# Attention and a routed feed-forward layer on one core: both norms applied by ScalarE, a router product on both weight parts at once, a new order of the attention blocks, and the last block's work between the first expert tiles

## The reference

```
x = x + xattn(layernorm(x), ctx)          # 16 heads of 32, softmax over the 154 context rows
x = x + moe(layernorm(x))                 # 8 experts of 512 x 512, the 2 best of each token

xattn: q = x Wq^T + bq; k, v = ctx Wk^T + bk, ctx Wv^T + bv
       softmax(q k^T / sqrt(32)) v, then Wo^T + bo
moe:   softmax(x W_router^T + b_router), its 2 largest weights kept,
       sum over these two of weight * (x W_e^T + b_e)
```

## Time and profile before

| | us |
|---|---|
| median of the runs | 1371.55 |
| the profiled execution | 1366.51 |
| its span, first to last instruction | 1364.8 |
| PE busy | 1227.5 (90%) |
| DVE busy | 860.4 (63%) |
| POOL busy | 883.1 (65%) |
| ACT busy | 636.1 (47%) |
| mean granted clock of TensorE | 0.953 |

### The profile page before, as it was taken

The page is one execution under the profiler, slowest core; times in us unless marked ns, Lnnn a source line. Parts: engine busy times, 40 slices in busy tenths (PEclk is TensorE's granted clock), DMA queues, the critical chain, the costliest instruction groups (busy, mean ns, idle before and its releaser), DMA issues. The chain is left out here.

```text
span 1364.8 us, 37333 instructions
## 1 busy us (share of the span) xinstructions
PE 1227.5 (90%) x11552; PEld 743.6 (54%) x11553; DVE 860.4 (63%) x1905; ACT 636.1 (47%) x914; POOL 883.1 (65%) x1124
## 2 busy tenths in 40 slices
PE   5696899999998999899999997777899999999997
PEld 3352666665665656666566565443455555555553
DVE  3363687877787678687688676744455555555544
ACT  2204557546655645754754753512333343433333
POOL 5112467878878878878878966966544555454445
PEclk9787899999999989999999998888999999999999
DMA  8814456537647647656654655677999999899786
GB/s 238 224 35 128 116 152 193 188 119 232 200 127 226 179 137 221 173 166 191 193 181 126 209 156 164 243 278 185 245 178 171 173 175 175 167 168 179 143 160 120
DMA packets 136024, 240.07 MB, mean 176 GB/s; under 512 B 18533, under 2 KB 49509, under 8 KB 134757
## 3 DMA queue, kind: packets, MB, share of 16 engines
q1 hardware_dynamic: 102432, 160.67, 40.1%
q0 software_dynamic: 29952, 67.73, 24.4%
q10 hardware_dynamic: 3525, 10.06, 2.0%
HBM read 113.34 MB, written 101.71 MB: 158 GB/s over the span
## 5 line engine op out<-in xcount | busy, mean ns | idle before, releaser
L1778 PE MATMUL S<-we_s,wq_s 128*128 x1632 | 379.5, 383 | 13.9 <-DVE wq_s L1734 5.8
L1711 POOL DMA_INDIRECT out<-xn,to x136 | 210.6, 1549 | 210.1 <-DMA out<-xn,to 80.6
L1111 POOL TENSOR_TENSOR we_s<-P_s,we_s 128x1024 f16<-128x1024 f32 x112 | 239.3, 2155 | 51.2 <-ACT we_s L876 25.5
L1778 PEld LDWEIGHTS S<-we_s,wq_s 128*128 128x128 f16 x1632 | 159.2, 99 | 183.6 <-issue 24.7
L1722 ACT ACTIVATE wq_s<-PVp 128x512 f16<-128x512 f32 x138 | 82.1, 596 | 238.6 <-PE PVp L1768 238.3
L925 DVE TENSOR_REDUCE mx_sb<-S 128x6 f32<-128x924 f32 x160 | 170.9, 1110 | 2.1 <-PE S L684 2.1
L702 PE MATMUL W<-wo_s,aT_hi 128*128 128x512 f16 x512 | 162.7, 384 | 3.6 <-DVE xR_s L935 2.1
L667 PE MATMUL W<-we_s,wq_s 128*128 128x512 f16 x512 | 162.2, 389 | 3.2 <-DVE we_s L913 1.6
L1202 POOL DMA_INDIRECT dispatched<-xn,idx x128 | 126.6, 989 | 47.6 <-issue 46.7
L1756 DVE SCALAR_TENSOR_TENSOR att<-S,be_s 128x512 f32<-128x512 f32 x136 | 94.1, 692 | 97.9 <-PE S L1778 97.0
L768 PE MATMUL PVp<-Vr,we_s 128*128 128x132 f16 x768 | 92.9, 234 | 42.9 <-POOL we_s L1111 42.2
(11 more groups left out here) (190 smaller groups left out, 2038.0 us busy)
## 6 DMA issues: line engine op xcount, KB each, us to landing
P_s<-dispatched SPq DMA_DIRECT2D x140, 260.5 KB, 3.6
we_s<-we_s SPq DMA_DIRECT2D x192, 128.0 KB, 4.0
be_s<-in_x SPq DMA_DIRECT2D x16, 1024.0 KB, 9.7
xR_s<-in_x SPq DMA_DIRECT2D x16, 1024.0 KB, 6.1
out<-xR_s SPq DMA_DIRECT2D x16, 1024.0 KB, 10.4
wst<-in_weT SPq DMA_DIRECT2D x16, 512.0 KB, 7.5
we_scratch<-wsp SPq DMA_DIRECT2D x16, 512.0 KB, 6.9
Kst<-k_scratch SPq DMA_DIRECT2D x16, 480.0 KB, 5.7
```

The source lines that it names most:

```text
L1111: e.tensor_tensor(Pst[1][:, r:r + 2, :], exps(n), Pst[0][:, r:r + 2, :], ALU.subtract).then_inc(pldp, 1)
L1711: e.indirect_dma_start(out, bass.IndirectOffsetOnAxis(ap=to[u][:, :], axis=0), yw[u % YW], None, bounds_check=N - 1, oob_is_err=False, com ...
L1778: m = e.matmul(Yp[:, u % 2, :], gT[u % 2][xp][:, k, :], we_s[:, bass.ds(n * WN + (wp * KC + k) * D, D)], start=(c == 0), stop=(c == 11))
```

## The change

Six things are done:

1. `NA` is removed from POOL. `act_apply` does the same on ACT, one instruction for each tile of tokens (`NX0` to `NX3` for the first norm, `NY0` to `NY3` for the second), with scale and offset as operands. The semaphore `nap` now counts four for each block, and the scatters also wait for it.
2. `LA` multiplies the high part of the input with both parts of the weights at once, 16 columns wide, and the low part with the high weights, 8 wide: 32 matmuls in place of 48. `RA` scales both halves, and `RC` adds them instead of copying.
3. `BX` is called once for each tile of tokens, so that its four instructions can stand apart.
4. All five slot lists, `BANK` and `HOLDERS` are replaced. The slot of PE now begins at `Q10`.
5. `EARLY` is 13: the first table is made one block earlier and covers 12 turns and not 13.
6. `Oe1` to `Oe3`, `SN`, `NC`, `RQ`, `NY`, `O3` to `O11` of the last block and the scatters of the last two are taken out of the slots and put between the first tiles, over two turns. SP loads four tiles before the last expert weights, and writes the empty rows one in each turn from the third to the tenth.

```
-EARLY = 14
+EARLY = 13
...
-    def pool_norm_apply(e, n, b, src, dst):
-        e.wait_ge(nco[n], b.at(NCO, NCO))
-        hold(e)
-        for j in range(NJ):
-            i = e.tensor_scalar(dst[:, j, :], src[:, j, :], nrm[n][:, 5, j:j + 1], nrm[n][:, 6, j:j + 1], ALU.mult, ALU.add)
-        i.then_inc(nap[n], 1)
+    def act_apply(e, n, b, j, src, dst):
+        e.wait_ge(nco[n], b.at(NCO, NCO))
+        e.activation(dst[:, j, 0:D], src[:, j, :], ACT.Identity, scale=nrm[n][:, 5, j:j + 1],
+                     bias=nrm[n][:, 6, j:j + 1]).then_inc(nap[n], 1)
...
         for j in range(NJ):
-            seqs = [t for k in range(KC) for t in split3(k)]
-            for n, (xp, wp, k) in enumerate(seqs):
-                m = e.matmul(W[:, bank, j * NE:(j + 1) * NE], xnT[xp][:, k, j * P:(j + 1) * P], wr_s[:, wp, k, :], ...
+            o = W[:, bank, j * 2 * NE:(j + 1) * 2 * NE]
+            for k in range(KC):
+                e.matmul(o.rearrange("p (l e) -> p l e", l=2), xnT[0][:, k, j * P:(j + 1) * P], wr_s[:, :, k, :], start=(k == 0), stop=False)
+            for k in range(KC):
+                m = e.matmul(o[:, 0:NE], xnT[1][:, k, j * P:(j + 1) * P], wr_s[:, 0, k, :], start=False, stop=(k == KC - 1))
```

The start of the expert stage, the part of PE:

```
-            slots(e, pe_slot, -2, 2, 4)
+            slots(e, pe_slot, -3, 1, 4)
+            for i in range(3, 6):
+                pe_O(e, LAST, i, LAST + (-(-2)))
             e.wait_ge(ld_t[0], 16)
+            e.wait_ge(nmd, 4 * NB)
+            pe_turn_rows(e, 0, 0)
+            pe_turn_rows(e, 0, 1)
+            for i in range(6, 12):
+                pe_O(e, LAST, i, LAST + (-(-2)))
             e.wait_ge(ld_ew, 16 * (NE + 1))
...
-            pe_LB(e, LAST, LAST + (-(-1)))
-            for u in range(TU):
+            pe_tile(e, 0, 0)
+            pe_LB(e, LAST, LAST + (-(-2)))
+            for u in range(1, TU):
                 pe_tile(e, 0, u)
-                if u == 3:
-                    pe_R(e, LAST, LAST + (-(-2)))
+                if u == 5:
+                    pe_R(e, LAST, LAST + (-(-3)))
```

More of the change, by code:

```diff
@@ L1179, in pool_RW, with pool_BX @@
         ch.end()
[L1181 to L1193, removed]
+    def pool_BX(e, b, j):
+        if b.first and j == 0:
             e.wait_ge(L["bo"], 48)
[L1195 to L1198 removed]
+        if j == 0:
+            e.wait_ge(ld_xR[b.par], b.half(16, 16))
+            hold(e)
+        e.tensor_tensor(xR[b.par][:, j, :], xR[b.par][:, j, :], bo_b[:, :], ALU.add).then_inc(p_bx, 1)
     def scatter(e, p, k):
@@ new lines, in pe_slot @@
+        if on_bm1:
+            pe_ST(e, bm1, 7, s)
+            pe_ST(e, bm1, 8, s)
+        if on_bp1:
+            pe_XT(e, bp1, 1, s)
+            pe_XT(e, bp1, 2, s)
+        if on_bm1:
+            pe_PV(e, bm1, 2)
+            pe_PV(e, bm1, 3)
+            pe_ST(e, bm1, 9, s)
+        if on_bm3 and not bm3.last:
+            pe_R(e, bm3, s)
+        if on_bm2 and not bm2.last:
+            pe_O(e, bm2, 3, s)
+        if on_bp1:
+            pe_XT(e, bp1, 3, s)
+        if on_bm2 and not bm2.last:
+            pe_O(e, bm2, 4, s)
+            pe_O(e, bm2, 5, s)
@@ new lines, in pe_slot @@
+        if on_b:
+            pe_MX(e, b, 0, s)
+            pe_MX(e, b, 1, s)
+        if on_bm2 and not bm2.last:
+            pe_O(e, bm2, 6, s)
+        if on_bp1:
+            pe_Q(e, bp1, 0, s)
+        if on_b:
+            pe_MX(e, b, 2, s)
+        if on_bp1:
+            pe_Q(e, bp1, 1, s)
+        if on_b:
+            pe_MX(e, b, 3, s)
+        if on_bm2 and not bm2.last:
+            pe_O(e, bm2, 7, s)
+        if on_b:
+            pe_MX(e, b, 4, s)
+        if on_bm2 and not bm2.last:
+            pe_O(e, bm2, 8, s)
@@ new lines, in pe_slot @@
+        if on_b:
+            pe_MX(e, b, 5, s)
+        if on_bp1:
+            pe_Q(e, bp1, 2, s)
+        if on_b:
+            pe_MX(e, b, 6, s)
+        if on_bm1:
+            pe_PV(e, bm1, 4)
+        if on_b:
+            pe_MX(e, b, 7, s)
+        if on_bp1:
+            pe_Q(e, bp1, 3, s)
+        if on_b:
+            pe_MX(e, b, 8, s)
+        if on_bm2 and not bm2.last:
+            pe_O(e, bm2, 9, s)
+        if on_b:
+            pe_MX(e, b, 9, s)
+        if on_bm2 and not bm2.last:
+            pe_O(e, bm2, 10, s)
@@ L1300, in pe_slot @@
+        if on_b:
+            pe_MX(e, b, 10, s)
+        if on_bm2 and not bm2.last:
+            pe_O(e, bm2, 11, s)
+        if on_bm1:
+            pe_PV(e, bm1, 5)
+        if on_b:
+            pe_MT(e, b, s)
+        if on_bp1:
+            pe_Q(e, bp1, 4, s)
+            pe_Q(e, bp1, 5, s)
+        if on_bm2 and not bm2.last:
+            pe_LB(e, bm2, s)
+        if on_bm1:
+            pe_PV(e, bm1, 6)
+        if on_b:
+            pe_ST(e, b, 0, s)
             pe_ST(e, b, 1, s)
@@ L1402, in pe_slot @@
[L1402 to L1432 removed]
+            act_EX(e, b, 1)
@@ L1532, in dve_slot @@
             dve_SN(e, bm1, 0)
-        if on_bm2 and not bm2.last:
-            dve_RE(e, bm2)
         if on_bp2:
```

458 lines of the change are left out of this document (213 added, 245 removed), and 8 rows, old and new, of the table BANK.

## The result

The changed kernel is slower by 1.5%: 1389.68 us median of four runs (1388.23 to 1396.53) against 1372.94 (1371.31 to 1376.96) of the kernel before beside it, ratio 1.0147 with a 95% interval from 1.0114 to 1.018. The forecast was 1313. The profiled executions are 1388.23 and 1366.51 us, 21.7 apart.

A forecast was written before the change was run, and what follows sets the result against it. PE's waits for POOL's low parts, from a latency chain and a full POOL queue, were taken as the limit. 1366.51 - 50.7 (slots) + 5 (start) + 4 (table) - 17 (last stretch) = 1307.8; with 5.04, 1313 us, range 1289 to 1348.

The forecast's parts named there:

- The slots: Stage of similar slots, 678.4 us: 13.7 x (49.5 - 44.3 - 1.5) = 50.7 us gained, between 7 and 71.
- The walk: Going through the new slot lists with the trace's durations: no wait over 0.5 us found.
- I take 1.5 us left over: Each slot: 1.5 us lost above PE's floor of 44.3 us, bounded by 0 and 4.7.
- 13.7 slots: The stage of 678.4 us counted as 13.7 slots of 49.5 us, all with the same gain.
- Rival 2: Slots: NX0 on ACT waits for NC(0) on POOL and delays MT's eviction; slower, 1388 us at 7 us late; chance 0.07.
- The start: First block: XT0 3.5 us later behind NX0 to NX3, plus WEh's load; 5 us lost, 0 to 10.
- WEh ahead of Qh0: Block 0: WEh now precedes Qh0, its load behind two others in SP's queue; 0 to 4 us.
- The table: First table's DVE instructions, 8.8 us, now in block 14's full slot: 4 us lost, 0 to 9.
- The last stretch and the first tiles: Behind the slots: O3 to O11, R and empty rows rearranged, 17 of 48 us back, 0 to 30.
- 20 us by their spacing: First tiles: both scatters of the last two blocks, 16 indirect DMAs, between POOL's adds, covered only by the adds' lag.
- these 3 MB are less than what the stretch moves in that time: Last three expert weights, loaded behind PV7: some 15 us of work before the first tile covers them.
- The rule on shared ports: Beside WEl in the slots: BX freed of 1.0 us, SD or PL0 charged if DVE slips; counted as nothing.

The follow-up runs named there:

- e4: Changed kernel with the last three expert weights' load back in front of SP's waits, on chip A: 1359.75 us, ratio 0.9961 to the kernel before.
- e9: Changed kernel unedited, as control on chip C: 1389.98 us, ratio 1.0165 to the kernel before.
- e10: Same kernel as e4 (weights' load back in its old place), on chip C beside e9: 1390.68 us, ratio 1.0166 to the kernel before.
- e8: Changed kernel with PE's ten looped slots as one pass of ten, without the jump back, chip B: 1382.97 us, ratio 1.0107 to the kernel before.
- e1: Changed kernel with both applied norms back on POOL, chip A: 1379.21 us, ratio 1.0098 to the kernel before.
- e6: Changed kernel with the first block's NX0 to NX3 issued earlier and XT1, XT2 changing banks, chip B: 1387.21 us, ratio 1.0143 to the kernel before.
- e7: Changed kernel with EARLY = 14, the first table one slot later as before, chip B: 1390.33 us, ratio 1.0161 to the kernel before.
- e3: Changed kernel with block 14's scatters and block 15's NC, RQ ahead of POOL's first add, chip A: 1349.89 us, ratio 0.9898 to the kernel before.
- e13: Changed kernel with the edits of e3, e4, e6, e7, e8, and POOL waiting for DMX9 before SC, chip D: 1362.03 us, ratio 0.9955 to the kernel before.
- e15: Changed kernel with e3, e6, e7, e8, the table's DMA ahead of the weights, SC waiting for DMX9, chip D: 1359.59 us, ratio 0.9944 to the kernel before.
- e17: As e15 without SC's wait, and with SC's four indirect DMAs ahead of PL9, chip E: 1336.59 us, ratio 0.9767 to the kernel before.
- e18: Same kernel as e15 (SC waits for DMX9), on chip E: 1360.09 us, ratio 0.9951 to the kernel before.
- e5: Changed kernel unedited, as control on chip B: 1390.17 us, ratio 1.0169 to the kernel before.

## Why the prediction was wrong

It missed by 80 us of difference: -58.7 forecast, +21.7 measured between the two profiled executions. About 20 us of it are due to the chip: e4, worth as much as the changed kernel where both ran (e9, e10), took 1359.75 on A, ratio 0.9961. So even on a chip without the stands the kernel would have come out some 47 us above the forecast, which is an estimate.

**The slots.** Forecast 50.7 us gained, 13.7 us gained from MT(0) to MT(14): 37 us of the miss. The walk itself was right on PE's waits. The first wait of PE (before PV0) is 0.4 to 0.6 us, the second (before PV2) is gone, the clock is 1.00 from 259.76 to 499.14. "I take 1.5 us left over" on a floor of 44.3 gave slots of 45.8; on chips A, D and E they are 45.7 to 45.8. Over MT(3) to MT(8), e4 has 228.82 us with 4.4 in listed waits, so the floor is 44.9 and what is left over 0.9: two errors of 0.6 that cancel. Three things were not in it.
- The stands of DVE at DMX7 to DMX9, 2.0 us a slot on three of the six sets of runs, the first among them: ten intervals by 1.95 are the 19.5 us that the ledger lacks. I had bounded what is left over by 4.7 a slot, but from waits of the walk. What causes the stands is open.
- "13.7 slots": the first three intervals, where PE waits mostly for DVE's low part and for the restack's DMAs (7.5 and 7.1 us at most in the changed kernel) and little for POOL (2.8 us before), gained nothing (+0.8 in place of 11.1 gained).
- PE's jump back: 3.39 us before, 5.08 after and in the middle of Q, with the clock at half behind it. The interval rose by 3.0, where a gain of 3.7 was counted. e8 shows what it is worth: 7.2 us. It was in the trace and in no term.

**Rival 2 did not hold.** The applies of both norms waited for NC on POOL 12.1 us in all, in 14 times, at most 1.7, and 0.65 for NX0 of the slot at 294.79. Where they are back on POOL (e1) the slot is longer. That the kernel is slower has nothing to do with ACT in POOL's loop.

**The start.** 5 forecast, 8.8 measured. The first misreading is of the earlier trace rows: 40.96 is the first eviction and not XT0, which began at 33.45. XT0 came at 45.20, just behind the forecast of 43 to 45, but 11.8 us later than before and not 3.5; the first eviction came 5.4 later. What I did not see: XT0 and XT1 share one bank now and XT2 and XT3 the other, which costs two waits of 1.41 us before the first Q. None of this is what the start lost, though. The step that was mis-sized is WEh ahead of Qh0, "0 to 4 us". ACT's timeline before, with Qh0, and after, with WEh and Qh0:

```profile
51.14 0.69 ACT L823 ACTIVATE we_s<-W,bqs 128x512 f16<-128x512 f32 x1 [5.78 <-PE W L667]
```

```profile
58.44 1.06 ACT L899 ACTIVATE wsp<-wst 128x1024 f16<-128x1024 f32 x1 [5.16 <-DMA wst<-in_weT]
...
60.81 0.67 ACT L832 ACTIVATE we_s<-W,bqs 128x512 f16<-128x512 f32 x1
```

Qh0 is 9.7 us later. It is at 60.20 in e1 and at 61.53 in e6, where XT0 came at 35.18 and 37.83: it waits for WEh's load whatever comes before.

**The table.** 4 forecast (of 0 to 9), 6.8 measured. From the first to the end of the last its instructions take 9.7 us, 8.9 before; of them, three of 128x8 elements last 2.05 us each (DVE's timeline), beside three PL of POOL of 2.1 us each:

```profile
820.98 2.05 DVE L1087 TENSOR_SCALAR tb<-tb 128x8 f32<-128x8 f32 x1
823.06 2.05 DVE L1089 TENSOR_SCALAR tb<-tb 128x8 f32<-128x8 f32 x1
825.14 2.04 DVE L1091 TENSOR_TENSOR took<-tb,scan 128x8 f32<-128x8 f32 x1
```

POOL's timeline beside it:

```profile
820.88 6.28 POOL L1120 TENSOR_TENSOR we_s<-P_s,we_s 128x1024 f16<-128x1024 f32 x3
```

Their neighbours of the same size take 0.17. e7 shows that the table costs about as much in the next slot, so its place was not the loss.

**The last stretch and the first tiles.** 17 forecast back, 19.8 lost: the other 37 us. This is the step that failed outright, and by its own words: both scatters between the adds, "20 us by their spacing", "with only the adds' lag as cover". I priced POOL's time and not its queue: NC and RQ stood behind scatters and adds, DVE's RB in order behind RQ, every later tile behind RB. The measured stand is 13.74 us on DVE, 13.61 on PE; e3 gives back 12: from the first expert matmul to the end it takes 446.8 us, where it was 452.0 before and 464.3 in the changed kernel. Before, RQ of block 15 was done ahead of the first add. The second is the weights, "these 3 MB are less than what the stretch moves in that time": the sum counted no wait for them. The bytes were right, the moment of issue was not. SP reached them at 911.01, behind tile loads that waited for the table (889.38 before). The wait of 7.13 us is this, and it is the 7.5 us ahead of the first expert matmul; but e9 and e10 show that the early load is no gain as long as the table's DMA stands behind the weights and O6 to O11 behind the rows. Which of the two costs how much was not tested apart. I had counted O6 to O11 there as a gain.

**The rule on shared ports.** The long BX of the earlier trace rows is gone (1272 ns median, 1297 at most). What came in its place is one of POOL's NC instructions, 128x4, of 202 ns median, which beside WEl takes up to 1006 (all of its line, ns min, median, max, first and last start):

```profile
L574 POOL TENSOR_TENSOR nrm<-nrm x32: 198/202/1006, 23.8 to 950.5; 128x4 f32<-128x4 f32 x32
```

By the Trainium skill, "GPSIMD Engine Reference", Key points, GpSimd meets contention on its shared SBUF interfaces with VectorE's instructions of two SBUF inputs; both traces agree, 1.0 us at BX before and 0.8 at NC after. It charged NC, not SD or PL0, and cost PE nothing that can be seen.

## What to carry to other kernels

Where work is moved in front of a phase that has its own handshakes, write down for each moved instruction what stands behind it in its engine's queue and who waits for that; the price is that stand, not the instruction's time. A wait in a ledger is only a candidate: three of the five that were taken away (the weights, the table, most of the start) came back at the next one in line, and only an edit run beside its control on one chip tells. This order's slot time differed by 4% from chip to chip, so a gain from such an order should be measured on more than one.

## What the runs showed of the hardware that was not expected

- The same program has slots of 45.8 us on one chip and 47.6 on another (e4, e10: 1359.75 and 1390.68 us), and the kernel before only 1365.23 and 1367.78. The visible difference is DVE's stands at DMX7 to DMX9, with MX7's result long there. In the changed kernel's first profile the slot without scatters of a block (DMX7 at 207.69) has none, and the first slot in which POOL issues SC (251.22 to 256.1, DMX7 at 254.11) has them:

```profile
207.03 0.74 DVE L922 SCALAR_TENSOR_TENSOR we_s<-W,bqs,we_s 128x512 f16<-128x512 f32 x1
207.69 3.20 DVE L934 TENSOR_REDUCE mx_sb<-S 128x6 f32<-128x924 f32 x3
...
251.98 0.74 DVE L922 SCALAR_TENSOR_TENSOR we_s<-W,bqs,we_s 128x512 f16<-128x512 f32 x1
254.11 1.12 DVE L934 TENSOR_REDUCE mx_sb<-S 128x6 f32<-128x924 f32 x1 [1.39 <-PE S L692]
```

  In the changed kernel's slots the stands also keep to the time of the scatters: in the slot up to MT(14) SC is issued 2.3 us sooner after MT than in the slot up to MT(12), and there is one stand of 1.92 us before DMX7 and none before DMX8 and DMX9, which come when SC is over. But the kernel before has its SC beside three maxima without a stand (340.76, 3.18 us for the three), and so has e4 on chip A with the same order. So the scatters may be a condition and are not shown to be the cause; why some chips have it stays open. The kernels that were to tell (e13, e15, e17, e18) ran on chips without.
- The jump back in PE's list cost 4.9 to 5.2 us of issue in the three profiles of the changed kernel, on at least two chips, and 8.6 us of the interval with the halved clock behind it (e5 against e8).
- Three small instructions of DVE in a row lasted as long as the 128x1024 instructions of POOL beside them: 2.05 us in place of 0.17. Each began about 0.1 us after one of them and ended within 0.1 us of its end.
- The first table's one small DMA, issued right behind 2 MB of weights on the same queue (895.30), landed at 905.51, 10.2 us later, and SP went on at 906.79.
